# Expert activation with the gate copied by ScalarE and multiplied in by GpSimd, in a reordered transformer block

## The reference

```python
logits = jnp.einsum('th,eh->te', x, gate_weight)            # 32 experts
probs = jax.nn.softmax(logits)
top_val, top_idx = jax.lax.top_k(probs, 8); top_val /= sum(top_val)
w_tg = jnp.einsum('tk,tkg->tg', top_val, one_hot(merge_groups[top_idx], 8))
h = jnp.einsum('th,goh->tgo', x, gate_up_proj[dominant_experts])
gate, up = jnp.split(h, 2, axis=-1)                          # 8 groups of 96
act = jax.nn.silu(gate) * up
y = jnp.einsum('tgi,ghi->tgh', act, down_proj[dominant_experts])
out = jnp.einsum('tg,tgh->th', w_tg, y)
```

## Time and profile before

| | us |
|---|---|
| median of 3 runs | 1096.62 |
| lowest and highest | 1093.07, 1107.65 |
| the profiled execution | 1096.97 |
| its span | 1095.0 |
| DVE, ACT, POOL busy in it | 771.5, 401.1, 412.7 |

### The profile page before, as it was taken

The page is one execution under the profiler, slowest core; times in us unless marked ns, Lnnn a source line. Parts: engine busy times, 40 slices in busy tenths (PEclk is TensorE's granted clock), DMA queues, the critical chain, the costliest instruction groups (busy, mean ns, idle before and its releaser), DMA issues.

```text
span 1095.0 us, 24777 instructions
## 1 busy us (share of the span) xinstructions
PE 1026.2 (94%) x9744; PEld 730.9 (67%) x9744; DVE 771.5 (70%) x1516; ACT 401.1 (37%) x723; POOL 412.7 (38%) x349
## 2 busy tenths in 40 slices
PE   6979989999999989999899999999999998999778
PEld 4646667766677667766677666776677666776456
DVE  5767687585957868677885859678686777857344
ACT  3334533254314443145332543144431453314310
POOL 1526442264505353154422644054441544226100
PEclk9989999999999999999999999999999999999979
DMA  6220000200002000200002000020002000010000
GB/s 191 58 88 2 2 1 1 68 2 2 1 4 67 2 1 1 69 2 2 1 1 69 2 2 1 2 69 2 1 1 69 2 2 1 1 49 2 1 1 20
DMA packets 22232, 23.59 MB, mean 22 GB/s; under 512 B 6314, under 2 KB 20138, under 8 KB 22130
## 3 DMA queue, kind: packets, MB, share of 16 engines
q1 hardware_dynamic: 22130, 22.02, 6.6%
HBM read 17.80 MB, written 4.21 MB: 20 GB/s over the span
## 4 chain that ended last, share of the span: by engine, by line
PE 82%; DVE 11%; issue 4%; ACT 2%; POOL 1%; DMA 1%; POOLq 0%; DVEq 0%; SPq 0%; ACTq 0%
PE ring L1131 17%; PE ring L981 12%; PE ring L982 10%; PE ring L983 10%; PE ring L1203 8%; PE av L1147 7%; PE ring L1107 6%; PE ring L1098 3%; DVE mcol L863 2%; DVE xr L902 1%; PE ring L1115 1%; PE ring L1192 1%; DVE prod L839 1%; PE av L1160 1%; PE ring L1042 1%
## 5 line engine op out<-in xcount | busy, mean ns | idle before, releaser
L672 ACT ACTIVATE pt<-ring 128x384 f32<-128x384 f32 (+1 forms) x384 | 170.9, 532 | 326.2 <-PE ring L1131 289.7
L562 POOL TENSOR_SCALAR_AFFINE_SELECT pt<-pt 128x512 f32<-128x512 f32 x128 | 79.4, 635 | 409.6 <-ACT pt L672 409.6
L863 DVE TENSOR_REDUCE mcol<-ring 128x1 f32<-128x128 f32 (+3 forms) x512 | 212.3, 483 | 19.3 <-PE ring L1107 18.1
L839 DVE TENSOR_TENSOR prod<-ring,table 128x1024 f32<-128x1024 f32 x128 | 155.4, 1219 | 93.1 <-PE ring L983 92.5
L1131 PE MATMUL ring<-rows 32*128 32x512 f32 (+3 forms) x3072 | 175.9, 330 | 9.4 <-ACT pt L672 4.9
L1131 PEld LDWEIGHTS ring<-rows 32*128 32x128 f32 x3072 | 130.4, 184 | 60.6 <-issue 35.0
L553 POOL TENSOR_TENSOR rows<-prod,rows 128x1024 fp32r<-128x1024 f32 x64 | 152.5, 2393 | 36.3 <-ACT rows L652 36.3
L546 POOL TENSOR_TENSOR prod<-prod 128x512 f32<-128x512 f32 x64 | 82.5, 1290 | 134.3 <-DVE prod L839 133.7
L652 ACT ACTIVATE rows<-prod 128x1024 fp32r<-128x1024 f32 x64 | 67.0, 1060 | 60.2 <-PE ring L1131 39.3
L1147 PE MATMUL av<-pt,vals 128*17 128x512 f32 (+3 forms) x1024 | 85.3, 439 | 3.2 <-POOL pt L562 3.2
L1131 PE MATMUL ring<-cont 32*128 32x512 f32 (+3 forms) x1024 | 85.6, 319 | 0.0
(11 more groups left out here) (162 smaller groups left out, 1624.4 us busy)
## 6 DMA issues: line engine op xcount, KB each, us to landing
xn<-x_dram SPq DMA_DIRECT2D x8, 512.0 KB, 4.1
xr<-x_dram SPq DMA_DIRECT2D x8, 512.0 KB, 4.2
out_dram<-xr SPq DMA_DIRECT2D x8, 512.0 KB, 3.2
gate_bc<-gates_scratch SPq DMA_DIRECT2D x8, 256.0 KB, 4.3
pt<-wmod_dram SPq DMA_DIRECT2D x1, 1536.0 KB, 6.6
pt<-gup_t_dram SPq DMA_DIRECT2D x16, 96.0 KB, 2.6
dn<-wu_t_dram SPq DMA_DIRECT2D x1, 640.0 KB, 10.1
xr<-wk_t_dram SPq DMA_DIRECT2D x1, 512.0 KB, 8.3
```

Of the source, the lines that this page charges most:

```text
L672: sc.activation(pt[:, PT_AT[n] + h * w:PT_AT[n] + (h + 1) * w], ps[:, 0:w], ACT.Exp, scale=SCALE).then_inc(exp_ready.sem, 1)
L839: ve.tensor_tensor(prod[:, s % PROD, :, :], ps[:, :].unsqueeze(1).broadcast_to([P, 2, S]), table[:, :, :], ALU.mult).then_inc(rotated.sem, 1)
L863: last = ve.reduce_max(mcol[:, q, h * HR + HD:h * HR + HD + 1], ps[:, at:at + (q + 1) * P], AX_X)
```

## The change

For each k, `gated` is gone. ScalarE, after tanh, also copies gate / 2 from PSUM to SBUF (`gcopy`), into one of two buffers in turn, and that copy frees the gate's PSUM bank. DVE multiplies tanh + 1 by up (`upped`). GpSimd, which reads no PSUM, multiplies the result by the copied half gate (`gmul`). DVE multiplies by the weights (`weighed`), now after `gmul`. A `gcopy` waits for the `gmul` two tiles before.

```diff
+        gate_at = [pt[:, FT * S:FT * S + S], room[:, 3, :]]
...
-                "gate": lambda: (gate_used, ahead, step[2]),
+                "gate": lambda: (gate_copied, ahead, step[2]),
...
+                    elif kind == "gmul":
+                        k = step[2]
+                        wait(pool, gate_copied, b, ahead, k)
+                        wait_alone(pool, up_used, b, ahead, k)
+                        pool.tensor_tensor(inner[:, k, :], inner[:, k, :], gate_at[k % len(gate_at)], ALU.mult)                            .then_inc(gate_multiplied.sem, 1)
...
+                    elif kind == "gcopy":
+                        k = step[2]
+                        wait(sc, value_added, b, ahead, NG * NST - 1)
+                        wait(sc, tanh_ready, b, ahead, k)
+                        wait_alone(sc, gate_multiplied, b, ahead, k - len(gate_at))
+                        ps = bank(part, PLACES[part][0][("gate", ahead, k)])
+                        sc.activation(gate_at[k % len(gate_at)], ps[:, :], ACT.Copy, scale=0.5).then_inc(gate_copied.sem, 1)
...
-                    elif kind == "gated":
-                        k = step[2]
-                        wait(ve, tanh_ready, b, ahead, k)
-                        ps, act = bank(part, PLACES[part][0][("gate", ahead, k)]), inner[:, k, :]
-                        ve.scalar_tensor_tensor(act, act, 1.0, ps[:, :], ALU.add, ALU.mult)\
-                          .then_inc(gate_used.sem, 1)
                     elif kind == "upped":
                         k = step[2]
-                        wait(ve, gate_used, b, ahead, k)
+                        wait(ve, tanh_ready, b, ahead, k)
                         ps = wait_full(ve, b, part, ("up", ahead, k))
                         act = inner[:, k, :]
-                        ve.scalar_tensor_tensor(act, act, 0.5, ps[:, :], ALU.mult, ALU.mult)\
-                          .then_inc(up_used.sem, 1)
+                        ve.scalar_tensor_tensor(act, act, 1.0, ps[:, :], ALU.add, ALU.mult).then_inc(up_used.sem, 1)
                     elif kind == "weighed":
                         k = step[2]
-                        wait(ve, up_used, b, ahead, k)
+                        wait(ve, gate_multiplied, b, ahead, k)
```

## The result

The changed kernel takes 1124.02 us (median of four runs, 1122.38 to 1125.59). The kernel before, on the same chip, takes 1095.78 us, so the ratio is 1.0236, with an interval of 1.0179 to 1.0293. Forecast were 1096.5 us and a range up to 1113. The change makes the kernel slower, and by more than the range held.

A forecast was written before the change was run, and what follows sets the result against it. TensorE, busy 1026.2 of 1095.0 us, was taken as the bound, with VectorE bounding the stretch. Terms -7.7 + 4.0 + 2.4 + 1.3 = 0.0 left the span at 1095.0; forecast 1096.5 us, range 1082 to 1113.

The forecast's parts named there:

- the stretch: From value.032's end to gate.00: gate.00 at 19.6 us instead of 23.5, 2.8 of it moved work; gain 1.1 an image.
- (a): Start of an image: score.000, directly behind maxima.010 without a rope block, waits for the reduces; net +0.5 us an image.
- (b): Attention: with rope.1000 gone between score.021 and maxima.031, maxima.031's last head waits for exp.021; +0.3 us an image.
- the second rival: Stretch: lo.101, directly behind pow2, holds norm2; turn2 and gate.00 come 2.2 us later, 1112 us; chance 0.25.
- (c): Last image: gate.00 ahead of the logits wants both halves of low2, so nothing starts until then; +1.25 us.
- the end of the chain: Experts into down: upped.05, gmul.05, weighed.05 end about 3.1 us after down.00 begins; cost 0, cover 1.3 us.
- The third rival: Experts' end: combine.111 ahead of gmul.04 and gmul.05 makes GpSimd late, 1 to 3 us an image, 1104 to 1120; chance 0.10.
- DVE's spared time goes into slack: Experts: the 4.1 us of DVE spared an image go nearly all into slack, forecast 1096.5 us; chance 0.50.

The follow-up runs named there:

- e7: e2b with norm1.1 on VectorE's queue moved behind rotate.0310: span 1084.7 us, ratio 0.9902 to the kernel before.
- e2b: The changed kernel with GpSimd beginning lo.101 only when norm2 is done: span 1099.9 us, ratio 1.0040 to the kernel before.
- e8: e7 with rope.0200 put back between maxima.010 and score.000: span 1084.3 us, ratio 0.9900 to the kernel before.
- e10: e8 with the logits ahead of the first gate block again in the last image: span 1079.6 us, ratio 0.9861 to the kernel before.
- e5: The new arithmetic of the experts in the order of the kernel before: span 1093.1 us, ratio 0.9999 to the kernel before.
- e9: e8 with the old arithmetic (gated on VectorE, no gcopy, no gmul): span 1082.9 us, ratio 0.9869 to the kernel before.
- e4b: The kernel before with lo.101 moved behind pow2.0 on GpSimd's queue: span 1091.4 us, ratio 0.9955 to the kernel before.
- e1b: The changed kernel with norm1.1 moved behind rotate.0300 on VectorE's queue: span 1109.7 us, ratio 1.0150 to the kernel before.

## Why the prediction was wrong

**What failed first: `norm1` was never walked.** The change part by part follows the stretch and the experts; the attention got only (a) and (b). In the list of steps `norm1.1` moved, on DVE's queue, from behind `rotate.0310` and `reduce.020` to behind `rotate.0211`. It waits for nothing there, so the move looked free. But who runs beside it has changed: e7 against e2b (the same kernel but for `norm1`'s place) is 82.19 against 84.59 in the attention, 2.4 us an image, and 15.2 us in the span. It was no rival and no term of the sum, so the range had no room for it beside `norm2`'s wait.

**What failed second: the weight of the second rival.** The rival named the place (lo.101 directly behind pow2), the mechanism and the price: 2.2 us. Measured are 2.1, from 18.8 to 20.9. I left it out of the sum since `norm2`'s form takes 409 ns for 256 elements, as long as a reduce of 256 from PSUM (417), and concluded that it might not use the ports that GpSimd's multiplications hold. That step is wrong: an instruction can take about as long as such a reduce when alone, and be held all the same. The row that spoke for the hold, L811 with 0.44 where the median is 0.172, was the same opcode, and should have counted for more than an argument from a rate. The Trainium skill, "VectorE: DVE Perf Modes", section "What auto-detection actually checks", puts a single-source float32 instruction within SBUF in the two-port mode. The trace agrees in that the instruction is held, not in its speed: the shortest took 0.40 us for 256 elements, hardly faster than the reduce from PSUM. The Trainium skill, "SBUF — State Buffer", section "SBUF: two separate sides", gives the ports that VectorE and GpSimd share to whoever is first, for its whole instruction. The durations agree: at most 2.48 us, as long as a `lo`, and in the median of `norm1` 1.38, as long as a half of `combine`.

The rival's 1112 us was still short by 12: `norm1` wasn't in it, and neither was the lower clock, which cost 1.5 us more in four of six stretches.

**The gain of the stretch was there, and twice the forecast.** With the hold gone, it takes 18.8 us; forecast was 19.6. The walk had `lo.100` begin at 7.0 and hold the second addition of `mixed` until 10.05; in e7 it begins 5.8 us after `value.032`, beside the first addition, and the second is done at 9.3. Against 21.1, before with equal work, the stretch is 2.3 us shorter, where 1.1 was forecast. Not all of it is idle time of PE, which falls from 3.1 us to 1.6 (18.80 less 17.17): about 0.4 is that my 23.5 for before came from one image, while half the images of before take 24.4, with a lower clock, as this window of it shows:

```profile
654.20:678.50 24.30, 21.46 (x136) 15.98 (x137) 22.59 (x39) 7.25 (x11) 10.09 (x8) 0.93 0.00 1
```

**(a), (b), (c).** (a) is 1.0 at its place, its upper bound, and 0.3 in the end (e8), for 0.5 forecast. (b): PE's wait of maxima for the exponentials, L1106 <- ACT pt L680, is 2.6 us in 8, 0.33 an image for 0.3 forecast. (c) is 0.85 by e10 for 1.25.

**The experts and the end of the chain.** Right to 0.1 us. Down in the chain of after (start, us), and then in its timeline, POOL and DVE, the last `gmul`, the two `lo` behind it and the last two `weighed`:

```profile
585.38 10.57 PE ring L1211 x48
```

```profile
586.41 1.27 POOL L547 TENSOR_TENSOR pt<-pt,room 128x512 f32<-128x512 f32 x1 [3.75 <-DVE pt L963]
587.63 4.67 POOL L561 TENSOR_TENSOR rows<-prod,rows 128x1024 fp32r<-128x1024 f32 x2
586.16 0.68 DVE L969 TENSOR_TENSOR pt<-pt,ring 128x512 f32<-128x512 f32 x1
587.80 0.69 DVE L969 TENSOR_TENSOR pt<-pt,ring 128x512 f32<-128x512 f32 x1 [0.96 <-POOL pt L547]
```

`weighed.05` ends at 588.49, 3.1 us after down began, as walked, and down takes its 10.57 us without a wait. The third rival, GpSimd late at the end of the experts, didn't happen.

**The sum against the runs.** Forecast were -0.3 us an image (-1.1 + 0.5 + 0.3); measured are +4.0. Of the 4.3 between, 2.4 are `norm1` and 1.9 the stretch: the hold 2.1 and the clock 1.0 in the mean, less the 1.2 by which the stretch without them is better than forecast (2.3 for 1.1). The clock's 1.0 is that of this execution; no experiment sets it by itself. That DVE's spared time goes into slack, the claim I gave as the forecast, was right in both orders (e5, e9). It was the order, made for that arithmetic, whose neighbours on GpSimd I had to read, step by step, for all that moved on DVE and not only for what the arithmetic touches.

The best versions here, e7 to e10, are 1.0 to 1.4% faster than before, by intervals that all lie below 1 and overlap each other, and 3.3 to 3.7% faster than after by their ratios; they keep the new order but for `norm1.1` and the start of `lo.101`.

## What to carry to other kernels

A TENSOR_SCALAR or a two-input instruction of VectorE that works within SBUF has, in these runs, a price that depends on what GpSimd runs at that time. When such a step or a GpSimd multiplication moves in an order, look up both neighbours in the trace, also where the step waits for nothing; a place right behind the instruction whose end starts GpSimd was the worst here, and the reduces from PSUM between the two were a good shield (e4b). And if an engine's busy time goes up while its work went down, look at the mean of each group by form before looking at any wait.

## What the runs showed that I had not expected

- A single-input float32 TENSOR_SCALAR within SBUF of 128x256, 0.40 to 0.41 us alone, takes up to 2.48 us beside GpSimd's TENSOR_TENSOR. Of instructions back to back on both engines one got through per GpSimd instruction: behind a first of 0.41, three took 1.38, 1.39 and 2.48 us beside 1.38, 1.34 and 2.43.
- The time held is counted as busy time of VectorE in the profile (64.6 us for 22.0 of work) and appears in no list of waits under GpSimd's name: PE waits for `xn` or `cont`.
- Not held beside the same multiplications: a reduce from PSUM (2.48 us for four, in e4b), a multiplication with one input in PSUM (the last `weighed`, 0.69 us from 587.80, beside the `lo` from 587.63) and, though within SBUF, the statistics of `mixed` (0.75 us for two from 676.52 in after, beside the `lo.100` from 675.78). That `lo` itself took 2.85 us, having begun beside the first addition of `mixed`.
- The arithmetic of the experts, 4.1 us of DVE an image, changes no stage by 0.1 us in either order, nor the time beyond its interval.
- The granted clock fell in four of these six stretches of after and in none of the six of e1b's profiled execution, with the same 2.4 us of idle time of PE ahead in both. Executions of one kernel differ in this too (e1b 0.983 and 0.977, before 0.963 to 0.985). Why was not found out.
